# Moving weight preparation of the expert stage and of the last stage into the attention stages before them

## The reference

```
x += xattn(LN(x), ctx)     # 16 heads of 64; LoRA merged into Wq, Wk, Wv, Wo; 4 image tokens
x += mixture(LN(x))        # 8 experts, the best 2 of 8 per token; w_in (8,256,512), w_out (8,512,256); gelu
x += xattn(LN(x), ctx)     # 8 heads of 64, keys of 192 features
x += bit_ffn(LN(x)):
       ws  = mean(|w|);  wq = clip(round(w / ws), -1, 1) * ws      # for w_gate, w_up, w_down, 1 MB each
       act_quant(a) = round(a * 127 / max|a|) * max|a| / 127       # per token
       h   = silu(act_quant(x) @ wq_gate) * (act_quant(x) @ wq_up)
       out = act_quant(h) @ wq_down
```

## Time and profile before

| what | us |
|---|---|
| median of three runs | 1034.25 |
| profiled execution | 1031.65 |
| its span, first to last instruction | 1029.8 |
| around the span | 1.85 |
| A: steps / tail | 56 to 456 / to 486 |
| M: up to the first expert product / all | 486 to 551 / to 672 |
| C: steps / tail | 709 to 912 / to 930 |
| F: up to the first product / all | 930 to 959 / to 1030 |

### The profile page before, as it was taken

One profiled execution on the slowest core, in us unless ns is written; L12 is line 12 of the kernel. 1 busy time (PEld: TensorE's weight loads), 2 busy tenths in 40 slices (PEclk: granted clock), 3 DMA queues, 4 the chain that ended last, 5 costly groups with the idle time before them and its releaser, 6 DMA issues. The chain is left out here.

```text
span 1029.8 us, 23468 instructions
## 1 busy us (share of the span) xinstructions
PE 831.7 (81%) x8808; PEld 507.9 (49%) x8808; DVE 755.0 (73%) x1515; ACT 711.9 (69%) x1183; POOL 624.1 (61%) x574
## 2 busy tenths in 40 slices
PE   4876999999999999977525999868788979961576
PEld 4533565556555656554223777523445555651243
DVE  5858888788878886774685555458989887728796
ACT  3387999899979998961542444336897979924674
POOL 2078677777777777851345666424787878924142
PEclk9999999999999999996557999977999999966798
DMA  8579999999999999990964889762999979953155
GB/s 252 192 135 174 157 177 181 181 167 179 184 179 168 171 175 170 174 174 3 247 243 98 183 186 186 144 235 51 182 195 179 187 141 184 184 98 128 37 113 133
DMA packets 504878, 167.96 MB, mean 163 GB/s; under 512 B 477728, under 2 KB 495328, under 8 KB 504736
## 3 DMA queue, kind: packets, MB, share of 16 engines
q1 hardware_dynamic: 501024, 156.25, 81.4%
q0 software_dynamic: 3744, 10.23, 3.5%
HBM read 37.04 MB, written 11.14 MB: 47 GB/s over the span
## 5 line engine op out<-in xcount | busy, mean ns | idle before, releaser
L475 POOL TENSOR_TENSOR A_PHL<-A_pr,A_PHL 128x508 f16<-128x508 f32 x256 | 293.7, 1153 | 93.7 <-ACT A_pr L755 93.3
L754 ACT ACTIVATE A_PHL<-A_ps,A_negmax 128x508 f16<-128x508 f32 x256 | 190.1, 743 | 16.4 <-DVE A_negmax L999 13.3
L755 ACT ACTIVATE A_pr<-A_ps,A_negmax 128x508 f32<-128x508 f32 x256 | 191.8, 749 | 0.0
L475 POOL TENSOR_TENSOR C_PHL<-C_pr,C_PHL 128x512 f16<-128x512 f32 x128 | 149.6, 1178 | 51.2 <-ACT C_pr L755 51.1
L999 DVE TENSOR_REDUCE A_negmax<-A_ps 128x2 f32<-128x1016 f32 x128 | 154.2, 1205 | 0.0
L600 PE MATMUL A_ps<-A_K,A_Q 64*128 64x512 f16 x768 | 106.6, 383 | 18.0 <-ACT A_pr L755 13.9
L618 PE MATMUL A_ps<-A_VH,A_PT 128*128 128x65 bf16 (+1 forms) x1024 | 107.2, 195 | 7.8 <-DMA A_PT<-A_PHL 7.8
L619 PE MATMUL A_ps<-A_VL,A_PT 128*128 128x64 f16 (+1 forms) x1024 | 107.1, 193 | 0.0
L620 PE MATMUL A_ps<-A_VH,A_PT 128*128 128x65 bf16 (+1 forms) x1024 | 107.0, 194 | 0.0
L618 PEld LDWEIGHTS A_ps<-A_VH,A_PT 128*128 128x128 f16 (+1 forms) x1024 | 94.4, 98 | 22.1 <-DMA A_PT<-A_PHL 11.1
L754 ACT ACTIVATE C_PHL<-C_ps,C_negmax 128x512 f16<-128x512 f32 x128 | 90.8, 709 | 18.1 <-DVE C_negmax L999 17.3
(11 more groups left out here) (344 smaller groups left out, 2317.1 us busy)
## 6 DMA issues: line engine op xcount, KB each, us to landing
A_PT<-A_PHL SPq DMA_TRANSPOSE x256, 3.4
M_raw<-in_L_ffn_w_in SPq DMA_DIRECT2D x4, 1024.0 KB, 8.3
M_raw<-in_L_ffn_w_out SPq DMA_DIRECT2D x4, 1024.0 KB, 8.7
C_yc<-routed_rows SPq DMA_DIRECT2D x8, 512.0 KB, 5.0
M_rows<-M_xhl SPq DMA_DIRECT2D x4, 512.0 KB, 9.1
out<-X SPq DMA_DIRECT2D x16, 128.0 KB, 2.0
X<-in_x SPq DMA_DIRECT2D x1, 1536.0 KB, 14.1
ct_split<-A_CT SPq DMA_DIRECT2D x4, 384.0 KB, 2.8
```

The costliest lines, as they stand in the source:

```text
L475: pool.tensor_tensor(PHL[:, e % PRING, 1, 0:KEYS], pr[:, e % RING, 0:KEYS], PHL[:, e % PRING, 0, 0:KEYS], ALU.subtract).then_inc(pl_ready. ...
L754: a.activation(PHL[:, e % PRING, 0, 0:KEYS], o, ACT.Exp, bias=nm[:, n % 4, h:h + 1])
L755: a.activation(pr[:, e % RING, 0:KEYS], o, ACT.Exp, bias=nm[:, n % 4, h:h + 1]).then_inc(p_ready.sem, 1)
```

## The change

Two classes hold the weights of a later stage. `ExpertWeights` gives 10 of the 16 expert weights (five of w_in, five of w_out) to the first attention. Each is loaded alone (512 KB, ring of two), and split in two halves of 512 columns: 20 copies on ACT and 20 subtractions on POOL, on the steps `HALF_AT` (9, 11, 13, 15, 25, 27, 29 of the batches 1 to 3). The other six are loaded in M with two transfers of 1.5 MB and split by ACT and DVE; POOL splits nothing there. To make room, parts of A's memory are placed otherwise (`side="right"`, `first_out`, `gap`), which moves no instruction.

`TernaryWeights` loads the last stage's weights on steps 24, 28 and 32 of C, sums |w| on DVE in six parts, has PE and DVE make the scales on step 55, rounds on ACT in step 65 and bounds and writes the first two weights on DVE in the tail; the third is left for F. The norm's statistics of the first 12 tiles are taken in C too (steps 54, 60, 65 to 67); F takes those of the last four, with the square root by Newton steps, behind the first `x_max`.

```
+    def half_high(self, a, j):
+        raw, hi, lo = self.half(j)
+        a.wait_ge(self.loaded[j // 2 % 2], 16 * (j // 4 + 1))
+        a.activation(hi, raw, ACT.Copy).then_inc(self.hi, 1)
+
+    def half_low(self, pool, j):
+        raw, hi, lo = self.half(j)
+        pool.wait_ge(self.hi, j + 1)
+        pool.tensor_tensor(lo, raw, hi, ALU.subtract).then_inc(self.split, 1)
...
+    LOAD_AT = {24: 0, 28: 1, 32: 2}
+    SUM_AT = (40, 42, 44, 46, 50, 52)
+    SCALE_AT = 55
...
+    def round(self, a):
+        a.wait_ge(self.scale, 1)
+        for k in range(3):
+            a.activation(self.raw[k][:, :], self.raw[k][:, :], ACT.Copy, bias=self.MAGIC,
+                         scale=self.wr[:, k:k + 1]).then_inc(self.rounded, 1)
...
+    HALF_AT = [b * U + u for b in range(1, B) for u in (9, 11, 13, 15, 25, 27, 29)][:2 * nxt.EARLY] if nxt else []
+    LOAD_AT = {HALF_AT[max(2 * k - 3, 0)] + (2 if k > 1 else 2 * k - 8): k for k in range(nxt.EARLY)} if nxt else {}
...
+                if ffn and n in ffn.LOAD_AT:
+                    ffn.load(sp, ffn.LOAD_AT[n])
...
+                if n in HALF_AT:
+                    nxt.half_low(pool, HALF_AT.index(n))
...
+                if g in HALF_AT:
+                    nxt.half_high(a, HALF_AT.index(g))
...
+                if ffn and g in STATS_AT:
+                    done = STATS_AT.index(g)
+                    wait(v, pj_free, JOB["y", done, QT - 1] + 1)
+                    normal(done * QT, (done + 1) * QT, 0)
+                if ffn and G + 2 <= g < G + 4:
+                    normal(0, TILES - QT, g - G - 1)
...
+                if ffn and g in ffn.SUM_AT:
+                    ffn.part_sum(v, ffn.SUM_AT.index(g))
+                if ffn and g in (G + 5, G + 10):
+                    ffn.bound(v, (g - G) // 5 - 1)
+                if ffn and g in (G + 8, G + 12):
+                    ffn.write(v, (g - G) // 4 - 2)
...
-            load_w(0)
-            turn_rows(0)
-            turn_rows(1)
-            load_w(1)
-            turn_rows(2)
-            turn_rows(3)
-            load_w(2)
+            for p in range(4):
+                turn_rows(p)
+            weights.load_rest(sp, 0, raw)
             for p in range(4, PAIRS):
                 turn_rows(p)
-            load_w(3)
+            weights.load_rest(sp, 1, raw)
...
-            for k in BY_POOL:
...
+            weights.low(v, 10, raw)
+            weights.low(v, 11, raw)
...
-            w_low(8, 2 * E)
+            for k in range(13, weights.PARTS):
+                weights.low(v, k, raw)
...
+            pool.wait_ge(nmean_ready, 1)
+            normalise(0, 2 * GRP)
             x_final(0)
+            normalise(2 * GRP, 3 * GRP)
             x_final(1)
+            pool.wait_ge(nmean_ready, 2)
+            normalise(3 * GRP, NT)
...
-            ln_act()
-            a.wait_ge(w_loaded[2].sem, w_loaded[2].base + 16)
-            a.activation(mag[2][:, :], raw[2][:, :], ACT.Abs, accum_out=wsum[:, 2:3]).then_inc(sums_ready, 1)
...
-            for t in range(TILES):
-                ln_stat(t)
-            ln_rest()
...
+            mean(0, NT - GRP)
+            w.bound(v, 2)
+            w.write(v, 2)
             x_max(0)
+            x_weights(0)
+            last_group()
             x_max(1)
-            v.wait_ge(sums_filled, 1)
...
+            x_weights(1)
```

More of the change, by code:

```diff
@@ L430, in _ @@
                     load_vwo(b)
+                if n in LOAD_AT:
+                    nxt.load(sp, LOAD_AT[n])
         @block.gpsimd
@@ L1394, in _ @@
         def _(a):
-            def w_high(first, last):
-                for k in range(first, last):
-                    W, e = PARTS[k]
-                    a.wait_ge(w_loaded[k // PAIR % SETS], 16 * (k // PAIR // SETS + 1))
-                    a.activation(W[0][:, e, :, :].rearrange("p c n -> p (c n)"), raw[:, k % RAWS, :], ACT.Copy).then_inc(w_hi, 1)
             def row_high(p):
@@ L1811, in _ @@
                 x_round(t)
-            a.wait_ge(w_scale, 1)
-            for k in range(3):
-                a.activation(mag[k][:, :], raw[k][:, :], ACT.Copy, bias=MAGIC, scale=wr[:, k:k + 1]).then_inc(w_rounded, 1)
             def silu(t, half):
@@ L1843, in _, with mean, last_group @@
             xc = Chain(v, x_chain)
-            v.memset(ones[:, :], 1.0)
-            v.memset(wsum[:, 3:4], 0.0)
-            for t in range(TILES):
-                ln_stat(t)
-            ln_rest()
-            v.tensor_scalar(nmean[:, :], stats["mv"][:, :, 0], -1.0, None, ALU.mult).then_inc(nmean_ready, 1)
+            def mean(first, last):
+                v.tensor_scalar(nmean[:, first:last], stats["mv"][:, first:last, 0], -1.0, None, ALU.mult).then_inc(nmean_ready, 1)
+            def last_group():
+                tiles = slice(NT - GRP, NT)
+                one, two, half_v = (stats[k][:, tiles] for k in ("ve", "sd", "tmp"))
+                y = stats["rstd"][:, tiles]
+                for t in range(NT - GRP, NT):
+                    last = v.bn_stats(stats["st"][:, t, :], X[:, t, :])
+                xc.link(last)
+                for t in range(NT - GRP, NT):
+                    last = v.bn_aggr(stats["mv"][:, t, :], stats["st"][:, t, :])
+                xc.link(last)
+                xc.link(v.tensor_scalar(one, stats["mv"][:, tiles, 1], EPS, None, ALU.add))
+                v.tensor_scalar(half_v, one, -0.5, None, ALU.mult)
+                xc.link(v.tensor_scalar(two.bitcast(I32), one.bitcast(I32), 1, None, ALU.logical_shift_right))
+                xc.link(v.tensor_scalar(y.bitcast(I32), two.bitcast(I32), -1.0, float(0x5F3759DF), ALU.mult, ALU.add))
+                for _ in range(3):
+                    xc.link(v.tensor_tensor(two, y, y, ALU.mult))
+                    xc.link(v.tensor_tensor(one, two, half_v, ALU.mult))
+                    xc.link(v.scalar_tensor_tensor(out=y, in0=one, scalar=1.5, in1=y, op0=ALU.add, op1=ALU.mult))
+                mean(NT - GRP, NT)
             def x_max(g):
```

314 lines of the change are left out of this document (161 added, 153 removed).

## The result

The changed kernel takes 1036.1 us (median of 19 runs), the kernel before 1029.5 in the same comparison (19 runs). The ratio is 1.0068, 95% interval 1.0046 to 1.0090: the change makes the kernel 7 us slower (4.7 to 9.3). I had forecast 1018 with a range of 1006 to 1030, gave slower 0.07 and no change (under 0.5%) 0.09.

The account below looks back on a forecast made before the run. PE was taken to bound A's batches, DVE's lists the heads of M and F. A +3.0, M −9.6, C +3.6, F −11.5 sum to −14.5 us: 1017.2 to 1019.8, stated as 1018, range 1006 to 1030.

Parts of the forecast that it names:

- 7.4 us a batch into 23 of slack: hidden: A: POOL's lower halves, 1.05 us each, were to cost nothing because POOL has 23 us to spare a batch.
- the paragraph on the rule: Two-input or double-port DVE operations and POOL instructions exclude each other; in M, 2.12 us against 0.18.
- DVE's subtractions of 128x512: A: operations POOL's lower halves might hold up by the exclusion; DVE's slack there is 19 us a batch.
- So that fits and I charge nothing: A: ten 512 KB loads delay transposes (6.3 us in place of 3.4) within a 12.7 us margin, so cost 0.
- My slower rival: A: loads and copies paid in full, 40 us in place of 3.0, total +22.5, 1054 us; loss from 17.5; chance .07.
- ACT's copies "+3.0": A: 20 upper-half copies on ACT, 0.15 us each charged as a mean, +3.0 us (0 to +11).
- The idle 1.07 us that I gave to step 15: A, second batch: ACT stood idle 1.07 us before its exponentials on step 15, so a copy fits there.
- M: −9.6 forecast: M, up to the experts: faster tables without POOL's splitting, one lower half less, earlier transposes; −9.6 us (−14 to −5.5).
- C: +3.6 forecast: C: added loads, sums, statistics and tail work, mostly hidden; +3.6 us (0 to +12).
- "+1.0" for the three 1 MB loads: C, steps 24, 28, 32: each load holds transposes a few us inside a margin of 4 steps; +1.0 us.
- C pays in full: Rival: DVE, not PE, sets C's steps where sums stand; 22.1 us in place of 3.6, 1036 us; chance .09.
- F: −11.5 forecast: F's start: first silu 19.4 us after DVE's start in place of 29.86, plus 1.0 at the second silu; −11.5 us.

Follow-up runs that it names:

- pool_beside_norm: Kernel before plus four unused POOL subtractions of 128x512 on A's steps 43, 45, 75 and 77: ratio 1.0076 (1.0043 to 1.0110), +7.8 us.
- no_lows: Changed kernel without POOL's 20 lower halves on A's steps, zeros written in A's tail instead: ratio 0.9993 to the kernel before, A's steps 408.5 us.
- no_loads: Changed kernel with only the first two of A's ten 512 KB loads: ratio 0.9973 to the kernel before, A's steps 407.5 us.
- copies_only: Changed kernel with ACT's 20 copies but two loads in A and no POOL lower halves: ratio 0.9919 to the kernel before, A's steps 398.5 us.
- before_third: Kernel before, unchanged, profiled a third time: A's prologue 53.3 us.
- only_last: Kernel before plus only the change's last-stage half (TernaryWeights), A and M as before: ratio 0.9999 (0.9956 to 1.0043), A's prologue 60.7 us.
- last_early: Kernel before plus only the last-stage half, its three loads moved to C's prologue: 1020.2 us against 1028.0, ratio 0.9921.
- padded twin: Kernel before plus an unused 1.5 MB off-chip tensor, profiled twice: ratio 1.0016 (0.9986 to 1.0047), A's prologue 61.2 and 55.2 us.

## Why the prediction was wrong

- "In a batch ... POOL 23 [us to spare]" and "7.4 us a batch into 23 of slack: hidden". This step failed, and is shown (pool_beside_norm, no_lows): the lower halves cost 6 to 9 us, and four like them on steps 43, 45, 75 and 77 alone cost 7.8. Slack of POOL says nothing of what its work does to DVE; slack of DVE (19 us a batch, on which I leaned at the end of the paragraph on the rule) says nothing either, because what is held up is a chain of nine short operations ahead of K's projection, and PE is the bound and waits for that. I had the rule, I had the row that shows it (2.12 against 0.18), I used it to credit M with 7.4 us, and did not look for the same short chains in the stage to which the work went. What I named there, "DVE's subtractions of 128x512", are the wrong operations: they took 0.68 to 0.69 us beside a half-low and without one, and one of their inputs is A_ps, where PE writes its products, not SBUF.
- "So that fits and I charge nothing" for the loads. Failed: 7 to 10 us for the eight that were taken out (no_loads, copies_only), 0.9 to 1.3 each. The four steps are 12.7 us from scores to products, but most of them are gone before the transposes are issued. In a profile of the kernel before (before_third; medians over steps 33 to 123) the second transpose of a step is issued 8.1 us after the step's scores start, lands at 11.8, and PE's products with it start at 14.7: 2.9 us to spare, and I had read that a load makes a transpose land 2.9 later. In the changed kernel the spare time is 1.4, and under 0.35 in 20 of the 91 steps (2 before); without the eight loads it is 2.7. My slower rival had this mechanism, at 2.9 a load and with 11 for the copies; its turning point of 17.5 us for A was nearly reached (17.1), by loads and POOL rather than loads and ACT.
- ACT's copies "+3.0": 1.0, inside the range of 0 to 11. The idle 1.07 us that I gave to step 15 is at step 11 of that batch; both take a copy.
- M: −9.6 forecast, −9.5 measured, term by term as worked out: 2.8 up to the tables (1.94 + 1.0), 6.6 behind (1.79 + 1.75 + 1.93 + 1.2).
- C: +3.6 forecast, +7.1. The term that was too small is "+1.0" for the three 1 MB loads: 4.3. The rest, 2.6, measured 2.8. My rival "C pays in full" stood at 1036, the time that was measured; that is chance, for its 22.1 us in C were 7.1.
- F: −11.5 forecast, −13.2. Right; the last four tiles' statistics took 5.6 us in place of 6.3, and the first maximum came 0.6 sooner.
- The prologue of A was not considered. All ten profiles with part of the change in A had 59.2 to 62.6 us; of the eight without it five had 53.3 to 55.2 and three 59.8 to 61.2. It takes 4.7 of the 7.0 us in the means. Its cause is open: no instruction in it differs, the loads land later, and one unchanged program showed both values. Yet all 12 profiles with any part of the change, only_last and last_early among them, had the slow value, against one of the six without any; that speaks for a link to the program, which no run here explains. Without the prologue the stages sum to +2.3, below the interval of the times (4.7 to 9.3).

So of the forecast, −14.5, 14.1 went in A's steps and 3.5 in C; M and F gave 1.6 more; A's tail took 0.3, the experts' stretch 0.5 and the prologue 4.7: +7.0.

## What to carry to other kernels

Work moved to an engine with slack must be laid beside the neighbours' short dependent operations, not beside their busy share: four POOL instructions of 1.15 us cost 7.8 us because they closed the one gap in which DVE's chain ran. A transfer that is hidden in bandwidth still pays in latency when the transposes behind it feed the bounding engine: 0.9 to 1.4 us each here. Count the time to spare from the landing of the transfer to its use, not from the start of the step. Where the profile shows a collision that a change will remove in one stage, look for the same pair of instructions in the stage that takes the work.

## What was not expected of the hardware

- A 128x4 operation on DVE took 0.16 us alone and 1.08 to 1.12 beside a POOL subtraction of 1.15; of nine in a chain three were caught.
- The same program's first loads differ by execution: with the kernel before and its padded twin a 1 MB load landed after 5.5 to 5.9 us four times and after 9.6 once.
- One chip took some 15 us longer for M's experts and C's prologue, in every kernel, with the other stages unchanged.
